# A two-layer post-norm decoder on one core: 14 of 16 query/key/value tiles projected ahead of self-attention instead of 10, and the rest spread thin

## The reference

```
def quat_norm(q, eps=1e-06):
    r, i, j, k = jnp.split(q, 4, axis=-1)
    n = jnp.sqrt(r * r + i * i + j * j + k * k + eps)
    return jnp.concatenate([r / n, i / n, j / n, k / n], axis=-1)
...
q = quat_norm(quat_linear(x, qW, qb))
k = quat_norm(quat_linear(x, kW, kb))
v = quat_linear(x, vW, vb)
...
scores = jnp.einsum('bthd,bshd->bhts', q_, k_) * scale
scores = scores + jnp.mean(jnp.sin(J[:T])) * 0.1
attn = jax.nn.softmax(scores, axis=-1)
out = jnp.einsum('bhts,bshd->bthd', attn, v_).reshape(B, T, D)
return quat_linear(out, oW, ob)
```

## Time and profile before

| | us |
|---|---|
| median of 3 runs | 861.75 (859.05 to 863.91) |
| the profiled execution | 861.56 |
| its span, first to last instruction | 859.8 |
| TensorE busy | 734.8 (85%) |
| ScalarE busy | 544.5 (63%) |
| VectorE busy | 538.2 (63%) |
| GpSimd busy | 194.6 (23%) |
| head, up to the first scores | 0 to 62.15 |
| self-attention, up to the last o_evac | 62.15 to 317.58 |
| everything else | 317.58 to 859.8 |

### The profile page before, as it was taken

The page is one execution under the profiler, slowest core; times in us unless marked ns, Lnnn a source line. Parts: engine busy times, 40 slices in busy tenths (PEclk is TensorE's granted clock), DMA queues, the critical chain, the costliest instruction groups (busy, mean ns, idle before and its releaser), DMA issues.

```text
span 859.8 us, 10888 instructions
## 1 busy us (share of the span) xinstructions
PE 734.8 (85%) x3876; PEld 404.4 (47%) x3876; DVE 538.2 (63%) x1177; ACT 544.5 (63%) x912; POOL 194.6 (23%) x231
## 2 busy tenths in 40 slices
PE   3939999999999989999699999568889899994396
PEld 2612222211111128987588888235444654441285
DVE  4781656662212119779721657887987677888886
ACT  3648888899999971424121341365877643598991
POOL 1641112240000002216000402384544300000013
PEclk9978999999999999999899999889999999997599
DMA  6311212222355420202053200002010000000002
GB/s 198 103 26 26 47 26 62 25 41 71 74 173 104 96 77 1 98 1 98 1 196 109 87 2 1 0 1 74 1 37 1 1 1 1 0 0 0 2 24 74
DMA packets 57373, 42.13 MB, mean 49 GB/s; under 512 B 36866, under 2 KB 54120, under 8 KB 57192
## 3 DMA queue, kind: packets, MB, share of 16 engines
q1 hardware_dynamic: 57176, 41.31, 17.4%
q10 hardware_dynamic: 144, 0.13, 0.1%
HBM read 28.59 MB, written 4.46 MB: 38 GB/s over the span
## 4 chain that ended last, share of the span: by engine, by line
PE 40%; ACT 25%; DVE 22%; POOL 5%; issue 5%; DMA 1%; SPq 1%; POOLq 0%; DVEq 0%; ACTq 0%
ACT arena L589 16%; PE banks L1937 7%; PE banks L1722 5%; PE banks L1710 5%; PE banks L1458 4%; DVE arena L996 3%; DVE arena L1004 3%; PE banks L1444 2%; PE banks L1480 2%; DVE arena L1288 2%; PE banks L1619 2%; PE banks L1837 1%; PE banks L1742 1%; ACT arena L767 1%; ACT arena L778 1%
## 5 line engine op out<-in xcount | busy, mean ns | idle before, releaser
L589 ACT ACTIVATE arena<-banks 128x1024 f32<-128x1024 f32 x256 | 240.0, 1069 | 22.6 <-PE banks L1458 12.9
L1458 PE MATMUL banks<-arena 128*32 128x512 f32 x1024 | 137.3, 608 | 3.4 <-DVE arena L958 1.8
L1444 PE MATMUL banks<-arena 64*128 64x512 f16 x512 | 92.6, 391 | 22.8 <-DMA arena<-arena 13.3
L371 POOL TENSOR_SCALAR arena<-arena 128x2 f32<-128x2 f32 (+1 forms) x38 | 12.8, 336 | 356.7 <-DVE arena L999 356.7
L1444 PEld LDWEIGHTS banks<-arena 64*128 64x128 f16 x512 | 21.3, 93 | 135.0 <-ACT arena L589 104.7
L1937 PE MATMUL banks<-arena 128*128 128x512 f32 x192 | 83.1, 593 | 1.1 <-DVE arena L1304 0.9
L958 DVE COPY arena<-banks 128x512 f32<-128x512 f32 x16 | 11.1, 692 | 113.1 <-PE banks L1458 113.1
L680 ACT ACTIVATE arena<-banks,arena 128x77 f32<-128x77 f32 x256 | 59.3, 370 | 23.3 <-DVE arena L1212 23.3
L1945 PE MATMUL banks<-arena 128*128 128x256 f32 x192 | 43.7, 392 | 26.8 <-ACT arena L788 26.8
L1722 PE MATMUL banks<-arena 128*128 128x256 f32 x256 | 58.6, 391 | 5.8 <-DVEq L1134 5.8
L1937 PEld LDWEIGHTS banks<-arena 128*128 128x128 f32 x192 | 36.2, 190 | 47.4 <-issue 43.4
(11 more groups left out here) (245 smaller groups left out, 1300.4 us busy)
## 6 DMA issues: line engine op xcount, KB each, us to landing
arena<-in_L_ffn_w SPq DMA_DIRECT2D x16, 1024.0 KB, 7.5
w_kept<-arena SPq DMA_DIRECT2D x3, 768.0 KB, 3.6
arena<-w_kept SPq DMA_DIRECT2D x3, 768.0 KB, 4.8
arena<-in_x SPq DMA_DIRECT2D x4, 512.0 KB, 8.8
out_x<-arena SPq DMA_DIRECT2D x3, 512.0 KB, 2.9
arena<-in_L_ffn_b SPq DMA_DIRECT2D x1, 1024.0 KB, 8.7
arena<-in_L_ffn_w_gate SPq DMA_DIRECT2D x1, 768.0 KB, 7.5
arena<-in_L_ffn_w_up SPq DMA_DIRECT2D x1, 768.0 KB, 9.2
```

What stands on the lines that cost most here:

```text
L589: act.activation(PT[kt % 2][:, half], PS[:, 2 * (n % 3):2 * (n % 3) + 2, :], ACT.Exp, scale=DH ** -0.5 / QK_UP ** 2).then_inc(sem("exp_don ...
L1444: mm = pe.matmul(bank(2 * (n % 3) + h), KT[u % 2][64 * h:64 * h + 64, P * kt:P * kt + P], QT[u % 2][64 * h:64 * h + 64, 512 * half:512 * h ...
L1458: mm = pe.matmul(PS[32 * j:32 * j + 32, 6, :], VS[w][:, kt, h, :], PT[kt % 2][:, half, h, :], start=(kt == 0), stop=(kt == TB - 1))
```

## The change

HT goes from 10 to 14. Tiles 0 to 7 take the old way in the head. Tiles 8 to 13 are only turned, projected, biased and their values copied out there; their biased queries and keys wait unnormalised in the output buffers of units 1 to 6 (`OSB[:, 1 + i]`, each written only at its unit's end). GpSimd and VectorE normalise and split them, tile 8 + u in unit u for u = 0 to 5, by `late_norm`, `late_qn` and `late_low`, without a projection. Only tiles 14 and 15 are projected within self-attention, tile 14 over units 0 to 2 and tile 15 over units 3 to 5: the turn is in the first step, and the six matmuls stand in steps 3, 6, 9, 12, 16 and 19 of each 24 (`SPREAD`). Both are normalised in unit 6. `stage` is cut in three, put between the last `biased` of the head. The core of the diff:

```
-HT = 10
-LATE = T - HT
+HT = 14
+SPREAD = {3: (0, 0), 6: (1, 0), 9: (0, 1), 12: (1, 1), 16: (0, 2), 19: (1, 2)}
...
-        qk_sb = [prj(2, NQ, DQ) for _ in range(3)]
+        ringed = [prj(2, NQ, DQ) for _ in range(3)]
+        waiting = [OSB[:, 1 + i].rearrange("p (m c d) -> p m c d", m=2, c=NQ) for i in range(HT - TB)]
+        qk_sb = {t: waiting[t - TB] if TB <= t < HT else ringed[t % 3] for t in range(T)}
...
-            for t in range(HT + 1):
+            for t in range(HT):
                 if t + 1 < HT:
                     x_evac(t + 1)
-                if 3 <= t < HT:
+                if t == TB:
+                    norm(TB - 1)
+                if 3 <= t < TB:
                     high(t - 3)
-                if t < HT:
+                if t < TB:
                     square(t)
-                    v_evac(t)
-                if t >= 1:
+                v_evac(t)
+                if 1 <= t < TB:
                     norm(t - 1)
+                if t in (TB - 1, TB):
+                    high(t - 2)
...
             def biased(t):
                 dve.wait_ge(sem("qk_mm"), t + 1)
-                if t >= 3:
+                if 3 <= t < TB:
...
             def attn_unit(u):
...
-                if u < LATE:
-                    late_biased(u)
-                if 1 <= u <= LATE:
-                    late_qn(u - 1)
-                if u < LATE:
-                    late_v(u)
-                if u + 1 < LATE:
-                    late_x(u + 1)
+                late = HT + u // 3
+                if late < T and u % 3 == 0:
+                    late_x(late)
+                if u < HT - TB:
+                    late_qn(TB + u)
+                if u == HT - TB:
+                    for t in range(HT, T):
+                        late_qn(t)
+                if late < T and u % 3 == 1:
+                    late_biased(late)
+                if late < T and u % 3 == 2:
+                    late_v(late)
...
             def attn_unit(u):
                 for kt in range(TB):
...
-                    if kt == TB - 1 and u + 1 < LATE:
-                        late_turn(u + 1)
+                    late, step = HT + u // 3, TB * (u % 3) + kt
+                    if late < T and step == 0:
+                        late_turn(late)
                     values(u, kt)
-                    if u < LATE:
-                        late_project(u, kt)
+                    if late < T and step in SPREAD:
+                        late_project(late, *SPREAD[step])
```

More of the change, by code:

```diff
@@ L387, in _ @@
             pool.wait_ge(sem("quat_b"), 1)
-            for t in range(HT):
+            for t in range(TB):
+                if t == TB - 1:
+                    low_part(TB - 4)
                 pool.wait_ge(sem("sq"), t + 1)
@@ L424, in late_low @@
                 ins.then_inc(sem("qk_lo"), 1)
-            for i in range(LATE + 1):
-                if i < LATE:
-                    late_norm(i)
-                if i >= 1:
-                    late_low(i - 1)
+            late_norm(TB)
+            for t in range(TB, T):
+                if t + 1 < T:
+                    late_norm(t + 1)
+                late_low(t)
             pool.wait_ge(sem("x_tr"), T)
@@ L554, in square @@
                     act.wait_ge(sem("n2"), t - 1)
-                act.activation(sq[t % 2], qk_sb[t % 3].rearrange("p m c d -> p (m c d)"), ACT.Square).then_inc(sem("sq"), 1)
+                act.activation(sq[t % 2], qk_sb[t].rearrange("p m c d -> p (m c d)"), ACT.Square).then_inc(sem("sq"), 1)
             def norm(t):
@@ L883, in stage, with stage_values @@
                 ins.then_inc(sem("ks"), 1)
+            def stage_values(u):
+                w = u % 2
+                if u == NP:
+                    dve.wait_ge(sem("v_evac"), T)
+                if u == 0:
+                    dve.wait_ge(sem("j_exp"), 1)
+                    dve.wait_ge(sem("const"), 9)
+                    dve.wait_ge(sem("v_evac"), TB)
+                    dve.tensor_scalar(bq4[:, 2], bq4[:, 2], ec, None, ALU.mult)
+                    for v in range(2):
+                        ins = dve.tensor_scalar(VS[v][:, :, :, DH:DH + 1], ones[:, 0:1, None, None].to_broadcast([P, TB, 2, 1]), ec, None, ALU.mult)
+                    link(ins)
                 if u >= 2:
@@ L979, in _ @@
                     dve.tensor_copy(Gm[0:LC], bank(6)[0:LC, 0:B * LC].rearrange("p (b l) -> p b l", b=B)).then_inc(sem("mem_g"), 1)
-                if 2 <= t < HT + 2:
+                if 2 <= t <= TB:
                     normed(t - 2)
-                if t >= HT:
-                    low_part(t - 3)
+                if t == TB:
+                    normed(TB - 1)
+                if t == TB + 1:
+                    low_part(TB - 1)
+                    stage_queries(0)
                 if t == TB + 2:
-                    stage(0)
-            late_x(0)
+                    stage_keys(0)
+                if t == TB + 3:
+                    stage_values(0)
             for u in range(UN):
@@ L1470, in late_turn, with late_project @@
                 mm.then_inc(sem("x_tr"), 1)
-            def late_project(i, kt):
-                t = HT + i
+            def late_project(t, k, m):
                 x = xTs[t % 2]
-                if kt == 0:
+                if m == 0 and k == 0:
                     pe.wait_ge(sem("xT"), t + 1)
-                if kt < 4:
-                    m, k = kt // 2, kt % 2
-                    mm = pe.matmul(bank(7)[:, D * m:D * m + D], x[:, k], Wq4[:, k, m, :], start=(k == 0), stop=(k == KD - 1))
-                    if kt == 3:
-                        mm.then_inc(sem("qk_mm"), 1)
-                if kt in (4, 5):
-                    k = kt - 4
-                    if k == 0:
-                        pe.wait_ge(sem("qk_biased"), t + 1)
-                    mm = pe.matmul(bank(7)[:, 0:D], x[:, k], Wq4[:, k, 2, :], start=(k == 0), stop=(k == KD - 1))
-                    if k == KD - 1:
-                        mm.then_inc(sem("v_mm"), 1)
+                if m == 2 and k == 0:
+                    pe.wait_ge(sem("qk_biased"), t + 1)
+                c = D * (m % 2)
+                mm = pe.matmul(bank(7)[:, c:c + D], x[:, k], Wq4[:, k, m, :], start=(k == 0), stop=(k == KD - 1))
+                if k == KD - 1 and m >= 1:
+                    mm.then_inc(sem(("qk_mm", "v_mm")[m - 1]), 1)
             def attn_unit(u):
```

71 lines of the change are left out of this document (27 added, 44 removed).

## The result

| | before | after |
|---|---|---|
| device time, median of 9 runs | 860.85 us (857.51 to 863.98) | 852.4 us (847.72 to 853.76) |
| profiled execution: time | 861.56 | 853.7 |
| profiled execution: span | 859.8 | 852.0 |

The ratio of the two is 0.9896, with a 95% interval of 0.9871 to 0.9922. The change is faster, by 8.5 us (7.8 in the profiled spans), where the prediction said 15.1 and 846.5. The time lies 0.9 us above the range.

What follows compares the result with a forecast made beforehand. Self-attention was taken as bound by ScalarE's exponentials, but by TensorE where late tiles are projected. Start 0.1, unit 0 4.03, units 1 to 5 14.31, less 3.3 for late work: 15.1 us off 861.56, so 846.5, range 841.5 to 851.5.

Steps and rivals of the forecast that it cites:

- VectorE in the units: Units 0 to 6: VectorE stays off the path; unit 6, with two `late_qn`, needs at most 14.7 us, cost 0.
- rival 2: The head gets longer, first exponential at 65: 848.8 us, or 850.6 with dearer late steps; chance 0.17.
- TensorE comes from a gap under 1 us ... and so at clock 1.00: Unit 0: at full clock and without late work it would end at 79.22 instead of 83.25, 4.03 us.
- The head's start: Start of self-attention: first exponential at 62.7 against 62.80 before, a gain of 0.1 us.
- TensorE is the bound there: Head from tile 10 on: only copies and biases left, TensorE takes 2.80 us a tile, done at 60.7.
- the ends, 0 and 5.1: Late work left in units 0 to 5: cost put at 3.3 us, from 0 (all absorbed) to 5.1.
- A lone late matmul: Units 0 to 5: each of twelve costs 0.23 us; two turns, in units 0 and 3, 0.5 for both.
- the twelve to fourteen: Sign: ScalarE idle some 0.2 us in twelve to fourteen places, and not in each step.
- Behind self-attention: After the last o_evac: nothing changed, cost 0, 542 us to the end as before.
- the ring's pace: Head: 3.29 us a tile from tile 4 to tile 9; if held to tile 13, first exponential at 65.
- Rival 3: VectorE becomes the bound at 17.0 us in each of units 0 to 5, 11.4 more: 858 us; chance 0.03.
- Rival 4: TensorE's gaps in units 0 to 5 drop its clock to 1.2 GHz: 899 us, over two units 864; chance 0.02.

Runs made afterwards that it cites:

- experiment 1: The changed kernel with GpSimd's four bias additions held until VectorE has laid out unit 8's values: 846.84 us, ratio 0.9817 to the kernel before.
- experiment 2: The kernel before with GpSimd's bias additions held until unit 6 is copied out, so they fall on unit 8's layout: 865.18 us, ratio 1.0048.
- experiment 8: experiment 7's kernel with GpSimd's squares and sums of tiles 8 and 9 held until unit 0's keys are laid out: 843.6 us, ratio 0.9787.
- experiment 6: The changed kernel with ScalarE's dummy exponential, and so its table load, moved into the head's loop behind tile 9's value copy: 849.77 us, ratio 0.9865.
- experiment 7: The changed kernel with the edits of experiment 1 and experiment 6 together, measured twice: 845.92 us and 845.42 us.
- experiment 4: The changed kernel with only the fourth of GpSimd's bias additions held until unit 8's layout is done: 845.14 us in one execution.

## Why the prediction was wrong

**The step that failed** is the one that let the units from 6 on be, "VectorE in the units", with its "It just fits, cost 0". It was argued by VectorE's own work in unit 6, down to which `late_qn` the low part of tile 14 meets, and there it held: o_evac had 0.85 us to spare. But the work that the change moves on GpSimd has something behind it, the four additions L433, and these weren't followed. They stand behind the low part of tile 15, and that behind its `late_qn`. Before, unit 6 had one `late_qn`, early in it; now it has two, and the second ends with the unit. So the o_evac of unit 6 and the layout behind it moved up by 185.72 - 171.25 = 14.5 us, the additions by 180.81 - 171.73 = 9.1 only: where they led the layout by 5.5 us, they now start together. The prediction even had the price: it cited the lock between the two engines, and asked about it for GpSimd's squares alone, against the products of unit 6 and, in rival 2, against the layout in the head. What it left out was the question where the *unmoved* instructions behind the moved ones land. Experiments 1 and 2 show it from both sides: in the profiles unit 7 loses 4.3 us when the collision is taken out of the change, and gains 3.6 when it is put into the kernel before. Of the 4.3 us some 2.8 are the keys that came late, and some 1.5 TensorE at half clock behind the wait.

**The second miss** is "TensorE comes from a gap under 1 us ... and so at clock 1.00". The gap of 13.27 us was gone as predicted, and so was the long stretch at 0.50. The prediction also had ScalarE's table load in front of the first exponential, at the right time, with scores ready before. It didn't carry this one step further: with all score buffers full, TensorE then idles for the table and the first exponential, 1.56 us. Cost: 18.35 against 17.08 us in unit 0, 1.3 us. With the table load early the wait was 0.68 or 0.69 us and the clock stayed at 1.00 in 60 to 74, in five profiles of five. With it late the wait was 1.56 us in all six, and the clock fell in four of them, among them the change (unit 0: 18.29 to 18.36 us), and stayed up in two (17.06, and 17.49 with the late matmuls in a row). So the cost is the clock's, and the wait of 1.56 us alone doesn't decide it.

**What held, and what was luck.** The head's start: 62.79 against 62.7, since the table load ate what TensorE won. That it fits so well is partly luck: tile 9 was projected from 45.74 and tile 10 from 48.67, 0.7 and 0.8 us ahead of the 46.4 and 49.5 of the prediction, and then "TensorE is the bound there" failed once, by the 1.01 us wait at tile 12 of experiment 8. Units 1 to 5 stand 75.44 - 73.35 = 2.1 us over late-free ones. Unit 0 in experiment 6 is 17.08 - (14.67 + 1.75) = 0.66 over. Together 2.75 where 3.3 was predicted, and far from the ends, 0 and 5.1. But the terms of this sum were off in both directions. A lone late matmul was put at 0.23 us and a turn at 0.25; units 1 and 4 give 0.09 for a matmul, units 2 and 5 0.24 for one with a first step among them, and unit 3 leaves (15.46 - 14.67) - 0.18 = 0.61 for its turn. ScalarE isn't late in each step; it idles 0.15 to 0.20 us in four places of units 1 to 5 and 0.41 and 0.90 in unit 0, fewer than the twelve to fourteen that were named as a sign. The time won before unit 6, 170.91 - 156.58 = 14.3 us, is the forecast's 15.1 less 1.3 for the clock in unit 0, plus 0.5 that the late work cost less than its 3.3.

**Behind self-attention** the stretch is 544.65 against 542.22 us. The code there is the same in all kernels of this study, and its length in 14 profiles lies between 539.27 and 544.71. The three whose attention is that of before have 542.22, 543.50 and 544.64; of the others experiments 1, 6 and 7 have 542.55, 543.16 and 543.64. These 2.4 us are the scatter of one execution and no cost of the change. Leaving them out, the change won 10.2 us in its profile against 8.5 in the medians, whose interval reaches from 6.7 to 11.1.

**The rivals.** None of the four is what happened. Rival 2's number, up to 850.6, came near for other reasons. One part of its mechanism is there, GpSimd's work on VectorE's layout in the head: copies of 2.17 us instead of 0.63 and TensorE's wait of 1.01 (experiment 8). But the ring's pace didn't go on to tile 13, and the first exponential didn't come later. Rival 3 named VectorE as the bound in units 0 to 5, where it waits for TensorE in all of them. Rival 4, the clock at half in the units, is seen in a small way: for 4 us in unit 0 and behind a 3.22 us wait in unit 7, never in units 1 to 5. There the clock was 1.00 with gaps in each step, so the rule of the Trainium skill that stood with it ("TensorE: Matmul & The Clock Gate", section "A second HAM failure mode: psum-queue depth-cycling") is not borne out by them.

**What stays open.** Why the clock fell in unit 0 in four of the six executions with the late table load, and not in the other two, isn't settled; nor is why it stayed down for one step more in unit 7 of experiment 6 than in the change. The first exponential started between 59.83 and 62.80 us in three executions with the head of before, and between 60.46 and 62.84 in six with the change's. In the change and in experiment 4 the head is the same, and they part before 22 us: TensorE waits 2.25 against 0.80 us for the copy of its third tile and then runs at a clock of 0.50 against 1.00. What held the copy wasn't followed. This is why experiments were read by stretches between two events and not by where these stood.

## What to carry to other kernels

When work is moved, the engines' lists don't move by the same amount. Write down for each engine the first few instructions *behind* the moved ones, with their length, by how much they shift and by how much the neighbour that shares a port shifts; here 9.35 us of additions that nobody waits for cost 4.3 us because they moved 9.1 us and the layout 14.5. Such filler work is best tied to an event (behind the layout) rather than left to start when it can, or cut into pieces of a length that the neighbour's slack can bear. And a fixed cost that sits in idle time, like a table load, has to be placed again when that idle time goes.

## What the runs showed of the hardware

A VectorE fp16 copy of 128x256 takes 0.16 us, 0.7 beside GpSimd additions of 128x256, and 2.33 beside ones of 128x1024: it waits for one whole instruction of GpSimd each time. VectorE's own instructions don't slow GpSimd much (the four additions took 9.35 us with the collision, 9.34 with half of it and 9.35 with none).

TensorE's granted clock can fall after a short gap. In the change 1.56 us without work, then work with gaps in it, was followed by 4 us at 0.52 and 0.63; the same gap in six kernels was followed by the fall in four and not in two, and a gap of 0.68 in none of five. In unit 7 a wait of 1.07 us left the clock at 1.00. Waits of 2.48, 3.22 and 3.29 us were each followed by `values` of 1.93 us instead of 1.07, and unit 7 grew by 1.5, 1.5 and 2.5 us beyond what the lateness itself explains.
